# Cross attention with a second, cross-channel attention: the order of the weight loads and of TensorE's work in the setup

## The reference, cut to what matters

```python
# x (4, 2048, 640); ctx (4, 154, 384): 150 rows of keys, then 4 conditioning rows; 8 heads of 80
query = x @ Wq;  keyt = enc @ Wk;  valt = enc @ Wv
hs = mha(query, keyt, valt)
ca_q1 = einsum('btc,th->bch', ca, Wq_ca)[:, indices, :]
ca_hs1 = mha(ca_q1, x, x)
ca_q2 = ca_hs1 @ Wq
ca_hs2 = mha(ca_q2, ca @ Wk_ca, ca @ Wv_ca)
out = (hs + ca_hs2) @ Wout + b_out + x
```

## Time and profile before

| | us |
|---|---|
| median of 3 runs (1532.04, 1533.33, 1535.11) | 1533.33 |
| the profiled execution | 1535.76 |
| its span, first to last instruction | 1534.0 |
| outside the span | 1.76 |
| the setup and the keys, up to the first transpose of x | 43.26 |

### The profile page before, as it was taken

One profiled execution on the slowest core, in us unless ns is written; L12 is line 12 of the kernel. 1 busy time (PEld: TensorE's weight loads), 2 busy tenths in 40 slices (PEclk: granted clock), 3 DMA queues, 4 the chain that ended last, 5 costly groups with the idle time before them and its releaser, 6 DMA issues.

```text
span 1534.0 us, 24564 instructions
## 1 busy us (share of the span) xinstructions
PE 1499.9 (98%) x10310; PEld 1246.0 (81%) x10310; DVE 789.5 (51%) x1596; ACT 622.5 (41%) x1311; POOL 2.8 (0%) x12
## 2 busy tenths in 40 slices
PE   7999999999999999999999999999999999999998
PEld 5764799999975489999987549999998745999998
DVE  6785435344478363444448726435345873453533
ACT  2438633333244852332332584323233377333322
POOL 0000000000000000000000000000000000000000
PEclk9999999999999999999999999999999999999999
DMA  6640011120252001140045100213004410021101
GB/s 237 225 156 1 7 57 66 57 110 27 104 192 95 1 20 52 57 157 18 27 149 176 57 1 20 90 37 148 9 35 165 172 37 2 19 95 57 61 18 44
DMA packets 46680, 117.28 MB, mean 76 GB/s; under 512 B 3661, under 2 KB 5317, under 8 KB 45019
## 3 DMA queue, kind: packets, MB, share of 16 engines
q1 hardware_dynamic: 37036, 93.91, 17.6%
q10 hardware_dynamic: 9535, 21.80, 3.7%
HBM read 77.33 MB, written 39.17 MB: 76 GB/s over the span
## 4 chain that ended last, share of the span: by engine, by line
PE 91%; DVE 4%; ACT 2%; issue 1%; DMA 1%; SPq 0%; ACTq 0%
PE ps_w L511 47%; PE ps_s L511 18%; PE ps_t L511 16%; PE ps_t L521 6%; PE ps_w L521 3%; DVE unit_max L1329 2%; ACT work L1133 1%; PE ps_s L521 1%; ACT ot L1047 0%; DMA xc<-in_L_xattn_Wv_ca_dram 0%; DMA xc<-in_x_dram 0%; DVE ca_mat L1345 0%; DVE ot L1441 0%; ACT ot L1116 0%; DVE xt_l L1355 0%
## 5 line engine op out<-in xcount | busy, mean ns | idle before, releaser
L511 PE MATMUL ps_w<-wo_h,ot 128*128 128x320 f32 x1280 | 310.4, 314 | 0.6 <-DVE ot L1441 0.6
L1329 DVE TENSOR_REDUCE unit_max<-ps_s 128x1 f32<-128x512 f32 x384 | 240.6, 683 | 54.6 <-PE ps_s L511 53.6
L1103 ACT ACTIVATE work<-ps_s,neg_max 128x150 f32<-128x150 f32 x512 | 152.1, 402 | 223.4 <-DVE neg_max L1387 223.4
L511 PEld LDWEIGHTS ps_w<-wo_h,ot 128*128 128x128 f32 x1280 | 220.2, 188 | 0.9 <-DVE ot L1441 0.9
L511 PE MATMUL ps_w<-wo_l,ot 128*128 128x320 f32 x640 | 197.4, 308 | 0.0
L511 PEld LDWEIGHTS ps_w<-v_all,work 120*128 120x128 f32 x1280 | 170.3, 190 | 3.1 <-issue 2.5
L511 PE MATMUL ps_w<-v_all,work 120*128 120x162 f32 (+1 forms) x1280 | 171.3, 288 | 0.0
L1383 DVE TENSOR_REDUCE neg_max<-ps_s 128x6 f32<-128x900 f32 x64 | 70.0, 1094 | 165.2 <-PE ps_s L511 165.2
L511 PE MATMUL ps_s<-keys_h,qt_h 128*128 128x300 f32 (+1 forms) x448 | 140.0, 312 | 0.0
L511 PE MATMUL ps_s<-keys_h,qt_l 128*128 128x300 f32 (+1 forms) x448 | 131.5, 293 | 0.0
L511 PE MATMUL ps_s<-keys_l,qt_h 128*128 128x300 f32 (+1 forms) x448 | 131.1, 293 | 0.0
(11 more groups left out here) (171 smaller groups left out, 2352.3 us busy)
## 6 DMA issues: line engine op xcount, KB each, us to landing
xc<-in_x_dram SPq DMA_DIRECT2D x32, 1280.0 KB, 6.4
out_dram<-work ACTq DMA_DIRECT2D x64, 320.0 KB, 2.2
xt_all<-work SPq DMA_DIRECT2D x60, 256.0 KB, 2.2
xt_l<-xt_all SPq DMA_DIRECT2D x12, 1280.0 KB, 5.6
y_all<-in_L_xattn_Wk_dram SPq DMA_DIRECT2D x4, 960.0 KB
y_all<-in_L_xattn_Wv_dram SPq DMA_DIRECT2D x4, 960.0 KB
pick<-pick_all SPq DMA_DIRECT2D x16, 194.0 KB
xc<-in_L_xattn_Wq_dram SPq DMA_DIRECT2D x1, 1600.0 KB, 10.7
```

The source lines that it names most:

```text
L511: return nc.tensor.matmul(out, lhs, rhs, start=start, stop=stop, skip_group_check=True)
L1103: return nc.scalar.activation(probs[:, h * KEYS:(h + 1) * KEYS], ps_s[:, bank, c * KEYS:(c + 1) * KEYS], exp, bias=neg_max[:, s % 2, h:h + ...
L1329: v.tensor_reduce(unit_max[:, a, n, q:q + 1], bank, AX_X, ALU.max).then_inc(max_free, 1)
```

## The change

The loads: Wq is now the first of the large ones, and Wk_ca and Wv_ca go behind it into the homes of Wk and Wv. So Wk and Wv can only be loaded when K2/V2 are done; they go behind Wout. PE turns Wq first, then makes K2/V2, turns them, makes M2, turns the context, makes VW2, and only then the keys. The four unread products are dropped. DVE splits Wq ahead of K2/V2's copies and makes `wo_l` ahead of the work on M2. ACT splits Wout ahead of the context's copy. SP waits for `gyw_first` before the second load of x.

```diff
-            sp.dma_start(wk_ca, Wk_ca.rearrange("(k p) n -> p k n", p=P)).then_inc(su_ca_in, 16)
-            sp.dma_start(wv_ca, Wv_ca.rearrange("(k p) n -> p k n", p=P)).then_inc(su_ca_in, 16)
             sp.dma_start(stage_w, Wq.rearrange("(k p) n -> p k n", p=P)).then_inc(su_wq_in, 16)
+            sp.dma_start(wk, Wk_ca.rearrange("(k p) n -> p k n", p=P)).then_inc(su_ca_in, 16)
+            sp.dma_start(wv, Wv_ca.rearrange("(k p) n -> p k n", p=P)).then_inc(su_ca_in, 16)
...
-                sp.dma_start(wk, Wk.rearrange("(k p) n -> p k n", p=P)).then_inc(kv_in, 16)
-                sp.dma_start(wv, Wv.rearrange("(k p) n -> p k n", p=P)).then_inc(kv_in, 16)
...
                 if b == 0:
                     sp.wait_ge(wq_ready, 1)
                     sp.wait_ge(wq_turned, KT)
                     sp.dma_start(stage_w, Wout.rearrange("(k p) n -> p k n", p=P)).then_inc(su_wout_in, 16)
+                    sp.wait_ge(kv2_full, 1)
+                sp.dma_start(wk, Wk.rearrange("(k p) n -> p k n", p=P)).then_inc(kv_in, 16)
+                sp.dma_start(wv, Wv.rearrange("(k p) n -> p k n", p=P)).then_inc(kv_in, 16)
+
+                if b == 0:
                     sp.wait_ge(gyw_ready, 1)
...
                     load_x(0, 0)
+                    sp.wait_ge(gyw_first, 1)
                     sp.wait_ge(gyw_out, 16)
                     load_x(1, 1)
...
-            pe.wait_ge(su_turned_ready, 1)
-            pe.wait_ge(su_ca_in, 16 * 2)
-            for c in range(CT):
...
-            last.then_inc(kv2_full, 1)
             pe.wait_ge(su_wq_in, 16)
             turn_wq(ps_t_flat, 0)
             turn_wq(ps_s_flat, 1)
             turn_wq(ps_w_flat, 2)
+            pe.wait_ge(wq_copied, 1)
+            turn_wq(ps_t_flat, 3)
+            pe.wait_ge(wq_copied, 2)
+            turn_wq(ps_s_flat, 4)
+
+            pe.wait_ge(su_turned_ready, 1)
+            pe.wait_ge(su_ca_in, 16 * 2)
+            for c in range(CT):
+                for r, (w, lo, hi) in enumerate(((wk, 0, CAD), (wv, 0, CAD), (wk, CAD, HID), (wv, CAD, HID))):
+                    last = mm(ps_w[32 * r:32 * (r + 1), 2, 0:hi - lo], ca_t[:, c, :], w[:, c, lo:hi], c == 0, c == CT - 1)
+            last.then_inc(kv2_full, 1)
             pe.wait_ge(kv2_copied, 1)
...
-            pe.wait_ge(wq_copied, 1)
-            turn_wq(ps_t_flat, 3)
-            pe.wait_ge(wq_copied, 2)
-            turn_wq(ps_s_flat, 4)
...
             turn_ctx(0)
-            pe.wait_ge(wq_ready, 1)
-            for n in range(UNREAD_SETUP):
-                mm(ps_w[:, 1, :], wq_h[:, n, 0:P], wq_h[:, n, 0:CHUNK], True, True)
+            pe.wait_ge(su_wout_in, 16)
+            for half in range(2):
+                for j in range(KT):
+                    last = mm(vw2_banks[half], v2_bd[:, j, :], stage_w[:, j, half * HALF:(half + 1) * HALF], j == 0, j == KT - 1)
+            last.then_inc(vw2_full, 1)
...
-                if b == 0:
-                    pe.wait_ge(su_wout_in, 16)
...
-                    last.then_inc(vw2_full, 1)
...
-            take_ctx(0)
             act.wait_ge(su_wout_in, 16)
             nc.scalar.activation(wo_h[:, :, :], stage_w, copy).then_inc(wo_high, 1)
+            take_ctx(0)
...
+            dve.wait_ge(su_wq_in, 16)
+            steps.done(v.tensor_copy(wq_h[:, :, :], stage_w))
+            v.tensor_tensor(wq_l[:, :, :], stage_w, wq_h[:, :, :], ALU.subtract).then_inc(wq_ready, 1)
+
             dve.wait_ge(kv2_full, 1)
...
-            dve.wait_ge(su_wq_in, 16)
-            steps.done(v.tensor_copy(wq_h[:, :, :], stage_w))
...
-            v.tensor_tensor(wq_l[:, :, :], stage_w, wq_h[:, :, :], ALU.subtract).then_inc(wq_ready, 1)
+            dve.wait_ge(wo_high, 1)
+            v.tensor_tensor(wo_l[:, :, :], stage_w, wo_h[:, :, :], ALU.subtract).then_inc(wo_ready, 1)
...
             base_columns(0)
-            dve.wait_ge(wo_high, 1)
-            v.tensor_tensor(wo_l[:, :, :], stage_w, wo_h[:, :, :], ALU.subtract).then_inc(wo_ready, 1)
```

More of the change, by code:

```diff
@@ L155 @@
 UNREAD = 4
-UNREAD_SUMS, UNREAD_SETUP = 3, 4
+UNREAD_SUMS = 3
 ALL_RUNS = range(7)
@@ L299, in cross_attention @@
         wq_t = [xc[:, KT + j, :] for j in range(3)] + [o_norm[:, :], probs_t[:, 5:10, :].rearrange("p a b -> p (a b)")]
-        wk_ca = work[:, 0:CT * HID].rearrange("p (k n) -> p k n", k=CT)
-        wv_ca = xc[:, KT:KT + CT, :]
         vw2_h, vw2_l = ot_h[:, 0, :], ot_l[:, 0, :]
@@ L535, in _ @@
             last.then_inc(su_turned, 1)
-            pe.wait_ge(su_turned_ready, 1)
-            pe.wait_ge(su_ca_in, 16 * 2)
-            for c in range(CT):
-                for r, (w, lo, hi) in enumerate(((wk_ca, 0, CAD), (wv_ca, 0, CAD), (wk_ca, CAD, HID), (wv_ca, CAD, HID))):
-                    last = mm(ps_w[32 * r:32 * (r + 1), 2, 0:hi - lo], ca_t[:, c, :], w[:, c, lo:hi], c == 0, c == CT - 1)
-            last.then_inc(kv2_full, 1)
             pe.wait_ge(su_wq_in, 16)
@@ L595, in _ @@
                 last.then_inc(k_full, 1)
-                if b == 0:
-                    pe.wait_ge(su_wout_in, 16)
-                    for half in range(2):
-                        for j in range(KT):
-                            last = mm(vw2_banks[half], v2_bd[:, j, :], stage_w[:, j, half * HALF:(half + 1) * HALF], j == 0, j == KT - 1)
-                    last.then_inc(vw2_full, 1)
                 pe.wait_ge(cst_base, b + 1)
```

## The result

The changed kernel takes 1538.40 us (median of 9 runs, 1535.09 to 1538.93) against 1533.57 us before (9 runs): a ratio of 1.0026 for runs compared side by side, 95% interval 1.0017 to 1.0035. It is slower, by a quarter of a per cent: the medians lie 4.8 us apart, the ratio gives 4.0 us. 0.4 us less was forecast. Beside later kernels the changed one was timed again: 1538.18, 1.0024 (1.0015 to 1.0034).

A forecast was written before the change was run, and what follows sets the result against it. TensorE and its waits bound the kernel; only the stretch to first x at 43.26 changes. Unread products -1.13, wait for x -0.44, context +1.20 sum to -0.37; -0.4 on the median 1533.33 gives 1532.9, range 1530.8 to 1536.4.

The forecast's parts named there:

- the one for the context: Setup, first batch: the context is turned at 26.8 instead of 25.60, adding 1.20 us to the way to first x.
- Wq's load and turns: Start of setup: Wq lands at 9.65, its 25 transposes take 5.4 to 15.1, Wout is issued at 15.2.
- K2/V2 at the high clock: K2/V2's products behind Wq's turns: they take 2.1 us instead of 4.05, since transposes come directly before.
- The fourth rival: K2/V2 and M2: transposes leave the clock low; first x +3.9, 1537.2 (all of M2 low: +6.9, 1540.2); chance 0.10.
- M2's end: M2's products in the setup end at 25.9, bounds 25.4 and 27.9; before the change 25.60.
- Wk and Wv at 26.8: Loads behind Wout: Wk and Wv land at 26.8, bounds 25.4 and 29.2; turn_ctx(0) waits for them.
- The price of that wait: Between M2's end at 25.9 and turn_ctx(0) at 26.8: only the later start was counted, no clock fall there.
- rival 1: Idle spells after K2/V2: the clock falls back, 3.2 us lost in M2; first x +1.9, 1535.3; chance 0.22.
- The unread products, -1.13: Behind the context's turns: dropping the four unread products saves 1.13 us on the way to first x.
- x no longer late, -0.44: Before first x: x, issued at 33.6, lands at 39.4, 3.5 early, so the 0.44 us wait goes.
- wo_l ahead of M2's work at nothing: VectorE makes wo_l from 24.7 to 28.2 ahead of M2's copies; these end at 29.9, 3.6 before the keys.
- the second: Wk and Wv's loads pay a start-up anew and land at 29.2; first x +2.0, 1535.4; chance 0.10.

The follow-up runs named there:

- the two versions with the warm clock: Context-in-gap kernel plus ten and eight unread identity products, 1533.15 us; and that with wo_l back behind M2's work and four more unread products, 1531.06 us.
- Wout, where it was last: Changed kernel with Wk and Wv issued ahead of Wout: 1539.10 us, ratio 1.0033 to the kernel before.
- the profile with the wait filled: Changed kernel with nine unread 128x512 products between M2 and the context's turns: 1536.30 us, ratio 1.0017 to the kernel before.
- the experiment on the kernel before: Kernel before the change with its four unread products left out and nothing else: 1535.42 us, ratio 1.0001.
- the version with the warm clock: Changed kernel, context's loads on their own semaphore, context turned behind K2/V2, ten unread identity products before Wq's wait and eight behind its turns: 1533.15 us.
- The versions with the wait removed or filled: Changed kernel with the context's three loads on their own semaphore, 1534.62 us; changed kernel with nine unread products before the context's turns, 1536.30 us.
- the keys-first version: Changed kernel with VW2's products moved back behind the keys: 1539.63 us, ratio 1.0034 to the kernel before.

## Why the prediction was wrong, step by step

The term that failed is the one for the context: +1.20 in the sum, +3.07 measured, and behind it a fall of the clock that the sum had at nothing and that cost 3.52. The other terms came as said.

- *What bounds it*: right. The first x was the point to watch, and its 4.97 us are the result (4.8 between the medians), with only small change behind it (1488.2 to 1489.1 in all profiles, the low clock taken off).
- *Wq's load and turns*: right. Wq landed at 9.94 (9.65 said), the turns took 5.6 (5.4 said; all of them at the slow rate), Wout was issued at 15.68 (15.2 said) and landed 6.5 later.
- *K2/V2 at the high clock*: right, 2.12 (2.1 said). The fourth rival falls: 25 transposes out of an idle stretch raised the clock. The Trainium skill, "TensorE: Matmul & The Clock Gate", section "Part 4: PE-mode transpose", says that transposes don't bring the full clock. This trace does not agree: passes that took 4.05 before took 2.12 with nothing but transposes in front.
- *M2's end*: 26.4 (25.9 said); the starts slipped by some tenths.
- *Wk and Wv at 26.8*: this step failed. Wv landed at 28.54, 1.7 later, and the context was turned at 28.67, past the 27.2 that the prediction had set as a sign of being wrong. The rate was as assumed; what was missing is a tail. In the changed kernel's windows the loads run at 402 GB/s to 26.5 and then trickle:
```profile
18.00:26.50 8.50, 6.49 (x53) 6.00 (x53) 4.18 (x13) 2.87 (x1) 0.00 (x0) 1.00 1.03 402
26.50:28.50 2.00, 0.00 (x0) 0.00 (x0) 2.00 (x1) 0.00 (x0) 0.00 (x0) 1.00 0.05 12
```
 A DMA share of 0.05 is about one of sixteen engines: it looks as if one had work left when all others were done. Between 25.5 and 26 us the queues show a load of instructions (one packet of 0.02 MB, 13.9% of the half microsecond's sixteen engines, so over one us of one engine), which could have held that engine back. The other traces fit: every version that loads Wout, Wk and Wv one behind the other has one such packet among them (at 18 to 20 us in the two versions with the warm clock, at 24 to 27 in the others) and the tail (Wv 10.1 to 10.55 from issue, Wout, where it was last, 11.91). The first three loads of the changed kernel have no such packet and no such tail: the share goes from 0.84 to 0.12 within half a microsecond (14.25 to 14.75). No run took the packet away, so the cause is argued and stays open.
- *The price of that wait*: this step failed too, and it made the size. The prediction had TensorE wait 0.9 us for the loads and put it at its length. It looked for a fall of the clock around K2/V2 (rival 1) and never at the new wait itself, which at 2.24 us was the longest idle time of TensorE since Wq. The fall cost 3.5 us, more than the wait. In the profile with the wait filled it is gone. That the wait's length alone decides is not shown: the clock fell behind a wait of 0.92 as well, and idle spells of 1.13 and 1.17 around K2/V2 stood before it.
- *The unread products, -1.13*: right for the changed order, where VW2 covers ScalarE's copy. In the old order they were worth nothing (the experiment on the kernel before).
- *x no longer late, -0.44*: right. *wo_l ahead of M2's work at nothing*: right here, with VW2 in front of the keys and TensorE late; it became the bound as soon as TensorE was early (the version with the warm clock), and with Wout late.
- Rivals: the second came nearest in its time of the load (29.2), not in its reason; the first exists and was seen in four profiles (0.66 to 0.70 over 20 to 25 us), but is not what was lost in this one. The fourth had the time that comes nearest (1537.2), by a mechanism that did not occur. The time, 1538.4, lies outside the range, which left out just the sum of a late load and a lost clock.

What stays open is how often the clock falls. The versions with the wait removed or filled have medians some 1.3 us above what their first x says (1534.6 with the first x 0.2 ahead of before's, 1536.3 with it 1.6 behind). A part of this is that the profiled execution of each was the fastest of its eleven runs. The rest goes with the clock: none of these 22 runs has a mean clock of 1.000, where 8 of the 35 of the kernel before beside them have. A fall in M2 in part of the executions would do it, and four profiles of versions with the new order show one. So the new order may cost some clock even without the wait; how often, no profile tells.

## What to carry to other kernels

Price a new wait on TensorE by its length and by the work that may follow at half clock: here 2.24 us of waiting were followed by a loss of another 3.5. Before comparing two profiles, take off what each lost at the low clock elsewhere. Split a semaphore that counts several loads before reordering them; the context needed three of the five, and one semaphore of its own gave back nearly the whole loss (1.0026 to 1.0005). When one buffer takes two loads in turn, follow the whole queue behind it: each cure here (Wout later, TensorE earlier) brought the next waiting instruction onto the path, VectorE's `wo_l` and then the load of x.

## What the runs showed of the hardware

- A transposing TensorE raises its clock as products do: blocks of five transposes at 1.07 to 1.33, and the products right behind at the fast rate (2.12 where 4.05 stood before). In the keys-first version the blocks themselves go from 1.07 to 0.93 and 0.55. The granted-clock column reads 1.00 over all of this (10 to 15 us), so this rise is read from the rates alone.
- An idle time of 2.24 us at 26.4 was followed by a granted clock of 0.50 over 30 to 35 us; with nine unread products in it the clock stayed. With four unread products behind the context instead, the idle time was 0.92 and the clock fell as well (0.50 over 30 to 32).
- The same program's runs differ by where the clock falls. Beside the last six kernels the kernel before ran, but for one run of 3536.4, 1531.5 to 1532.7 at a mean clock of 1.000, 1533.1 to 1534.4 at 0.999, 1534.6 to 1535.7 at 0.998, and 1536.3 to 1536.7 at 0.996 to 0.997. A difference of one or two us between medians is therefore partly a difference in how many executions meet such a stretch.
